# Attention probabilities in 384 columns instead of 512: the first 64 queries keep 64 keys, and their high and low parts share a transposed tile

## The chip, the core and the metric

The kernel runs on one core of a Trainium2 chip. TensorE does the matrix products, VectorE (DVE in the profile), ScalarE (ACT) and GpSimd (POOL) the elementwise work, and the DMA engines move and transpose data; SyncE (SP) issues nearly all DMAs. The metric is the device time of one execution in microseconds (us), lower is better.

## The reference

One transformer layer over 64 batch elements of 128 tokens and width 1024. Its input h comes from a token mixing stage (an S4 kernel) that isn't touched here. With `ln` for a layer norm:

```python
q = rope((ln(h) @ Wq).heads(32))          # head width 32
k = rope((ln(h) @ Wk).heads(8))           # 4 query heads share a key head
v = (ln(h) @ Wv).heads(8)
scores = q @ k.T / sqrt(32)
scores = where(key > query, lowest, scores)   # causal
h = h + softmax(scores) @ v @ Wo
logits = ln(h) @ Wr.T + br                # 8 experts of rank 16
h = h + 2 * einsum(ln(h) @ A.T, B, 8 * softmax(logits))
```

Since it is causal, the first 64 queries of an element see at most the first 64 keys.

## The kernel before

`s4_stage` makes h and stores it to HBM, and converts the weights. `layer_stage` does the layer, one batch element (128 tokens on the 128 partitions) at a time. Products are done in float16 with each operand split into a high part and a low part (the rounding's remainder), in three products: high with high, high with low, low with high.

Every engine runs its own list of steps, written out by hand: `body(i)` for i from -3 to 66, with steps for several elements at once (queries and keys of i+1 and i+2, attention of i, output projection of i-1, experts of i-2 and i-3). Nothing is reordered at run time: an engine takes its steps in this order, and each step first waits on semaphores (`reached`, `landed`). The order of TensorE's body is fixed in `body` at lines 1005 to 1048.

Attention goes by groups: group g (0 to 7) is one key head with its four query heads. Its steps are:

- `scores(b, g)`, TensorE, line 924: four matmuls into one PSUM bank. A tile is one half h of the queries (64) of a pair of heads, side by side on the 128 partitions. Tiles with h = 0 have 64 columns of keys, tiles with h = 1 have 128. `TILES` gives each of the four its place in a row of 512 columns.
- `mask_min`, VectorE, line 1207: mask and row minimum, tile by tile, into `pr`. It waits until `p_low` of group g - 2 has left `pr`.
- `exps`, ScalarE, line 1063: exponential and row sums, tile by tile.
- `reciprocals`, VectorE, line 1215: 1 / row sum, four a partition.
- `normalise`, GpSimd, line 1428: all 512 columns of `pr` times the reciprocals. Columns 64 to 127 of the h = 0 tiles hold zeros, set once.
- `p_high`, ScalarE, line 1073: the high part in float16 into `p16`; it waits (`landed`) until the DMA transpose of group g - 2 has read `p16`.
- `p_low`, GpSimd, line 1436: the low part, next to it.
- `p_transpose`, SyncE, line 862: a DMA transpose of the 1024 columns of `p16` into eight tiles `pt` of 128 x 128.
- `values(b, m)`, TensorE, line 939, twice an element, for groups 4m to 4m + 3: three rounds (v_hi with p high, v_lo with p high, v_hi with p low). A round has four matmuls of 512 columns, one a group, each with 32 weight columns on its own strip of 32 columns of the array. They add up in the bank `pv_ps`.
- `ctx_high` (ScalarE, line 1081) and `ctx_low` (VectorE, line 1221) split `pv_ps` into `ctx_t` (tiles 0 to 7 high, 8 to 15 low), which the output projection `wo_half` uses. Its blocks with k of 4 and more wait for `ctx_low(b, 1)`.

V itself comes from `kv_rotate` (VectorE) through `v_high` (ScalarE) and `v_low` (GpSimd, line 1476). Other steps named below: `norm_apply` (ScalarE, line 1099, a layer norm applied), `x_high` (ScalarE, line 1112) and `x_low` (VectorE, line 1268) split the activations; `sum_k` (GpSimd, line 1463) adds the two parts of the rotated keys; `q_double` and `k_double` (VectorE, lines 1307 and 1315) are float16 copies. In VectorE's body the steps around the change stand in this order:

```python
                    x_low(1, i - 2, 1)
                    mask_min(i, 3)
                    reciprocals(i, 2)
                    if i >= 0:
                        x_low(0, i + 2, 1)
                    reciprocals(i, 3)
                    ctx_low(i - 1, 1, 1 - odd)
```

and in GpSimd's, around the same time: `normalise` 0 and 1, `p_low` 0 and 1, `sum_k`, `normalise` 2 and 3, `p_low` 2 and 3.

Of the kernel before, what the change touches and what calls it, by code (L numbers as in the profile page):

```python
# [14 lines left out]
f16 = mybir.dt.float16  # L15
ALU = mybir.AluOpType
ACT = mybir.ActivationFunctionType
AX = mybir.AxisListType

P = 128  # L20
# [4 lines left out]
H, G, HD = 32, 8, 32  # L25
HG = H // G
# [8 lines left out]
RP = 4  # L35
# [31 lines left out]
HT = T // 2  # L67
# [574 lines left out]
def layer_stage(nc, h0, out, W, h_sent, ln_in):  # L642
# [5 lines left out]
    with ExitStack() as ctx:  # L648
        def sb(name, shape, dt=f32):
            return ctx.enter_context(nc.sbuf_tensor(name, shape, dt))  # L650

        def sem(name):
            return ctx.enter_context(nc.semaphore(name))

        def ps(name):
# [23 lines left out]
        ks = sb("ks", [P, G, 2, 2, HD], f16)  # L679
        kt = sb("kt", [P, G, P], f16)  # L680
        vf = sb("vf", [P, G * HD])
        v_hi = [sb(f"v_hi{i}", [P, G * HD], f16) for i in range(2)]
        v_lo = [sb(f"v_lo{i}", [P, G * HD], f16) for i in range(2)]
        smin = [sb(f"smin{i}", [P, HG]) for i in range(2)]
        pr = [sb(f"pr{i}", [P, HG * P]) for i in range(2)]
        rsum = [sb(f"rsum{i}", [P, HG]) for i in range(2)]
        rinv = [sb(f"rinv{i}", [P, HG]) for i in range(2)]
        p16 = [sb(f"p16{i}", [P, 2 * HG * P], f16) for i in range(2)]
        pt = [sb(f"pt{i}", [P, 2 * HG, P], f16) for i in range(RP)]
        ctx_t = [sb(f"ctx_t{i}", [P, 2 * G, P], f16) for i in range(2)]  # L690
        h1 = [W[f"rows{i}"][:, :, :].rearrange("p t l -> p (t l)") for i in range(2)]
        z8 = sb("z8", [P, NF])
# [10 lines left out]
        pv_ps, pa, pb, pc, pd, tx = (ps(n) for n in ("pv_ps", "pa", "pb", "pc", "pd", "tx"))  # L703
# [19 lines left out]
        ph_done = sem("ph_done")  # L723
# [9 lines left out]
        vh_done = sem("vh_done")  # L733
        masked = sem("masked")
        rinv_done = sem("rinv_done")
# [13 lines left out]
        k_sum = sem("k_sum")  # L749
        kl_done = sem("kl_done")  # L750
        vl_done = sem("vl_done")
        p_norm = sem("p_norm")

        TILES = tuple((h, pair, slice((2 * h + pair) * P, (2 * h + pair) * P + (HT, P)[h]))
                      for h in range(2) for pair in range(HG // 2))

        def in_halves(bank):
            return bank[:, :].rearrange("p (h j q) -> p h j q", h=2, j=HG)
# [1 line left out]
        def in_tokens(buf, k):  # L760
            return buf[:, k:k + HG, :].rearrange("p j (h q) -> p h j q", h=2)

        def has(b):
            return not isinstance(b, int) or 0 <= b < NB

        def reached(eng, s, per, b, k=0):

            if isinstance(b, int):
                if b < 0 or per * b + k == 0:
                    return  # L770
                if b >= NB:
                    b, k = NB, 0
            eng.wait_ge(s, per * b + k)
# [13 lines left out]
        with nc.Block() as block:  # L787
# [103 lines left out]
            def _(pe):  # L891
# [36 lines left out]
                def values(b, m, odd):  # L928
                    if not has(b):
                        return  # L930
                    if m == 0:
                        reached(pe, vl_done, 1, b, 1)
                    reached(pe, ctxl_done, G // 4, b, m)
                    for g in range(4 * m, 4 * m + 4):
                        landed(pe, b, g)
                    for n, (v, lo) in enumerate(((v_hi[odd], 0), (v_lo[odd], 0), (v_hi[odd], HG))):
                        for g in range(4 * m, 4 * m + 4):
                            strip = slice(HD * (g % 4), HD * (g % 4) + HD)
                            last = pe.matmul(pv_ps[strip, :], v[:, g * HD:(g + 1) * HD],  # L939
                                             pt[g % RP][:, lo:lo + HG, :], start=(n == 0), stop=(n == 2))  # L940
                    last.then_inc(pv_done, 1)

                def kv(b, odd, k0, k1):
# [110 lines left out]
            def _(act):  # L1054
# [12 lines left out]
                def p_high(b, g):  # L1067
                    if not has(b):
                        return
                    reached(act, p_norm, G, b, g + 1)  # L1070
                    pb_, pg = group(b, g - 2)
                    landed(act, pb_, pg)
                    A.activation(p16[g % 2][:, 0:HG * P], pr[g % 2][:, :], ACT.Copy).then_inc(ph_done, 1)  # L1073

                def ctx_high(b, m, odd):
                    if not has(b):
# [62 lines left out]
                def v_high(b, odd):  # L1139
                    if not has(b):  # L1140
                        return
                    reached(act, kv_used, 1, b, 1)
                    reached(act, pv_done, G // 4, b - 1)
                    A.activation(v_hi[odd][:, :], vf[:, :], ACT.Copy).then_inc(vh_done, 1)

                def router_exp(b):
                    if not has(b):
# [49 lines left out]
            def _(dve):  # L1197
# [13 lines left out]
                def reciprocals(b, g):  # L1211
                    if not has(b):
                        return
                    reached(dve, exp_done, G, b, g + 1)
                    V.reciprocal(rinv[g % 2][:, :], rsum[g % 2][:, :]).then_inc(rinv_done, 1)  # L1215

                def ctx_low(b, m, odd):
                    if not has(b):
                        return
                    reached(dve, ctxh_done, G // 4, b, m + 1)  # L1220
                    V.tensor_tensor(in_tokens(ctx_t[odd], G + 4 * m), in_halves(pv_ps),  # L1221
                                    in_tokens(ctx_t[odd], 4 * m), ALU.subtract).then_inc(ctxl_done, 1)

                def norm_half(w, src, b, half):
                    V.bn_stats(bn[w][:, 6 * half:6 * half + 6], src[:, 512 * half:512 * half + 512]).then_inc(ln_v[w], 1)
# [143 lines left out]
                def body(i, odd):  # L1369
# [3 lines that stand above are left out]
                    if i >= 0:  # L1373
                        x_low(0, i + 2, 1)
                    reciprocals(i, 3)
                    ctx_low(i - 1, 1, 1 - odd)
                    ls_low(i - 3)
                    mask_min(i, 4)
                    mask_min(i, 5)
                    reciprocals(i, 4)  # L1380
                    residual2(i - 3, 0, 1 - odd)
                    norm1_stats(i + 3)
                    residual2(i - 3, 1, 1 - odd)
                    reciprocals(i, 5)
                    q_double(i + 1, 0)
                    q_rotate(i + 1, 1)
                    residual1(i - 1, 0, 1 - odd)
                    mask_min(i, 6)
                    residual1(i - 1, 1, 1 - odd)
                    mask_min(i, 7)  # L1390
                    k_double(i + 1)
                    reciprocals(i, 6)
                    router_max(i - 2)
                    reciprocals(i, 7)
                    norm_refine(1, i - 1)
                    router_weights(i - 2)
                    norm_refine(0, i + 3)
                    if i == -3:
                        first_apply()
                    mask_min(i + 1, 0)  # L1400
                    mask_min(i + 1, 1)
                    q_double(i + 1, 1)
                    reciprocals(i + 1, 0)
                    x_low(1, i - 1, 0)
                    ctx_low(i, 0, odd)
                    reciprocals(i + 1, 1)
                    if i < -1:
                        x_low(0, i + 3, 0)
                        x_low(0, i + 3, 1)
                    kv_rotate(i + 2)  # L1410
                    q_rotate(i + 2, 0)
                    mask_min(i + 1, 2)
                    if i >= -1:
                        x_low(0, i + 3, 0)


                for i in range(2):
                    V.memset(pr[i][:, :].rearrange("p (t k) -> p t k", t=HG)[:, 0:2, HT:P], 0.0)
                bodies(dve, body)

            @block.gpsimd
            def _(pool):
                def normalise(b, g):
                    if not has(b):
                        return
                    reached(pool, rinv_done, G, b, g + 1)
                    p3 = pr[g % 2][:, :].rearrange("p (j k) -> p j k", j=HG)
                    nc.gpsimd.tensor_tensor(p3, p3, rinv[g % 2][:, :].unsqueeze(2).broadcast_to([P, HG, P]),  # L1428
                                            ALU.mult).then_inc(p_norm, 1)

                def p_low(b, g):
                    if not has(b):
                        return
                    reached(pool, ph_done, G, b, g + 1)
                    p = p16[g % 2]
                    nc.gpsimd.tensor_tensor(p[:, HG * P:], pr[g % 2][:, :], p[:, 0:HG * P],  # L1436
                                            ALU.subtract).then_inc(pl_done, 1)

                def sum_q(b, half):

# [31 lines left out]
                def v_low(b, odd):  # L1472
                    if not has(b):
                        return
                    reached(pool, vh_done, 1, b, 1)
                    nc.gpsimd.tensor_tensor(v_lo[odd][:, :], vf[:, :], v_hi[odd][:, :], ALU.subtract).then_inc(vl_done, 1)

                def body(i, odd):
                    v_low(i, odd)
# [59 lines left out]
```

## Time and profile before

| | |
|---|---|
| time, median of 3 runs | 2348.03 us (2345.55 to 2348.85) |
| the profiled execution | 2350.26 us, span 2348.1 us |
| granted TensorE clock, mean | 0.989 |
| TensorE busy | 2231.6 us, 95% |
| TensorE weight loads | 1147.6 us, 49% |
| VectorE busy | 1818.7 us, 77% |
| ScalarE busy | 1760.8 us, 75% |
| GpSimd busy | 1750.0 us, 75% |

The span is the time from the first to the last recorded instruction. The first stage takes some 250 us; from 330 to 2250 us the layer stage is full, one body after another. Matmuls are pipelined: the recorded duration of one is longer than its distance to the next, so distances between starts are what counts on TensorE. The other engines also begin an instruction some 0.1 us before the end of the one before it is recorded.

### The profile page before, as it was taken

The numbers are of one execution on the slowest core, as the hardware profiler recorded it, in microseconds if no ns is written. First come the engines' busy times: TensorE is split into PE (matmuls) and PEld (weight loads), VectorE is DVE, ScalarE is ACT, GpSimd is POOL, SyncE is SP. The second block draws the span as 40 slices with busy tenths as digits, with TensorE's granted clock in tenths as the row PEclk, the third lists the DMA queues.
The fourth block names the chain that finished last, engine by engine and source line by source line (L and its number), as shares of the span: only waits on it lengthen the run. The fifth ranks groups of instructions, "written<-read, shape, count | busy, mean of one in ns | idle before, by whom it ended". The sixth has DMA issues, their size and how long they took to land.

```text
span 2348.1 us, 49641 instructions
## 1 busy us (share of the span) xinstructions
PE 2231.6 (95%) x14040; PEld 1147.6 (49%) x14040; DVE 1818.7 (77%) x7750; ACT 1760.8 (75%) x6141; POOL 1750.0 (75%) x1550
## 2 busy tenths in 40 slices
PE   3898699999999999999999999999999999999986
PEld 2777344444444444444444444444444444444442
DVE  8999467777777777777777777877777777777864
ACT  5787477777787777777777777777778777778772
POOL 3776387777777778777778778788777777778772
PEclk9999899999999999999999999999999999999988
DMA  3888599999999999999999999999999999999994
GB/s 95 268 268 259 126 176 181 193 188 186 194 194 186 189 196 181 195 193 186 192 194 188 187 191 192 188 195 191 186 197 190 189 192 192 181 196 192 190 166 105
DMA packets 1205661, 443.10 MB, mean 189 GB/s; under 512 B 1155718, under 2 KB 1158022, under 8 KB 1205388
## 3 DMA queue, kind: packets, MB, share of 16 engines
q1 hardware_dynamic: 1205380, 439.93, 95.9%
q8 instruction: 113, 1.85, 0.3%
q14 instruction: 160, 1.31, 0.2%
q10 hardware_dynamic: 8, 0.01, 0.0%
HBM read 87.43 MB, written 67.11 MB: 66 GB/s over the span
## 4 chain that ended last, share of the span: by engine, by line
PE 67%; DMA 6%; POOL 6%; DVE 4%; SPq 3%; issue 2%; ACT 2%; POOLq 0%; DVEq 0%; ACTq 0%
PE pc L910 11%; PE pb L910 10%; PE pa L910 10%; DMA pt<-p 4%; PE pb L896 4%; PE pb L898 4%; PE pb L897 4%; PE pa L896 4%; PE pa L897 4%; PE pa L898 4%; PE pv_ps L939 3%; PE s_ps L924 3%; POOL p L1436 3%; POOL pr L1428 2%; DMA h_ln<-h 2%
## 5 line engine op out<-in xcount | busy, mean ns | idle before, releaser
L1063 ACT ACTIVATE pr<-pr,smin 128x64 f32<-128x64 f32 (+1 forms) x2048 | 738.8, 362 | 185.3 <-DVE smin L1207 184.4
L1428 POOL TENSOR_TENSOR pr<-pr,rinv 128x512 f32<-128x512 f32 x512 | 577.0, 1137 | 367.8 <-DVE rinv L1215 366.8
L1436 POOL TENSOR_TENSOR p<-pr,p 128x512 f16<-128x512 f32 x512 | 590.9, 1158 | 66.6 <-ACT p L1073 64.6
L1207 DVE CUSTOM_DVE_ANT_0 pr<-s_ps,cst 128x64 f32<-128x64 f32 (+1 forms) x2048 | 404.2, 252 | 219.0 <-PE s_ps L924 119.0
L1073 ACT ACTIVATE p<-pr 128x512 f16<-128x512 f32 x512 | 320.1, 625 | 257.8 <-DMA pt<-p 133.6
L1063 ACT ACTIVATION_READ_ACCUMULATOR pr<-pr,smin 128x1 f32 x2048 | 382.3, 187 | 0.0
L910 PE MATMUL pa<-wkv_hi,xt 128*128 128x512 f16 x1024 | 326.5, 380 | 13.4 <-DMA xt<-xs 13.4
L910 PE MATMUL pb<-wq_hi,xt 128*128 128x512 f16 x1024 | 326.9, 381 | 0.0
L910 PE MATMUL pc<-wq_hi,xt 128*128 128x512 f16 x1024 | 315.2, 379 | 0.0
L635 PE MATMUL hps<-z,xw 128*128 128x256 f32 x792 | 178.8, 386 | 60.5 <-POOL xw L363 38.2
L896 PE MATMUL pa<-wo_hi,ctx_t 128*128 128x512 f16 x512 | 195.5, 382 | 2.0 <-DVE ctx_t L1221 1.8
L910 PE MATMUL pb<-wq_lo,xt 128*128 128x512 f16 x512 | 195.4, 382 | 0.0
L897 PE MATMUL pa<-wo_lo,ctx_t 128*128 128x512 f16 x512 | 195.2, 381 | 0.0
L898 PE MATMUL pa<-wo_hi,ctx_t 128*128 128x512 f16 x512 | 195.2, 381 | 0.0
L910 PE MATMUL pa<-wkv_lo,xt 128*128 128x512 f16 x512 | 194.8, 381 | 0.0
L896 PE MATMUL pb<-wo_hi,ctx_t 128*128 128x512 f16 x512 | 194.7, 380 | 0.1
L898 PE MATMUL pb<-wo_hi,ctx_t 128*128 128x512 f16 x512 | 194.7, 380 | 0.0
L897 PE MATMUL pb<-wo_lo,ctx_t 128*128 128x512 f16 x512 | 194.7, 380 | 0.0
L910 PE MATMUL pc<-wq_lo,xt 128*128 128x512 f16 x512 | 194.2, 379 | 0.0
L635 PEld LDWEIGHTS hps<-z,xw 128*128 128x128 f32 x792 | 151.0, 193 | 87.9 <-POOL xw L363 44.2
L924 PEld LDWEIGHTS s_ps<-kt,qt 128*128 128x128 f16 x2048 | 121.8, 98 | 127.4 <-DVE smin L1207 22.5
L924 PE MATMUL s_ps<-kt,qt 128*128 128x64 f16 (+1 forms) x2048 | 172.0, 207 | 7.4 <-issue 4.1
(185 smaller groups left out, 4723.5 us busy)
## 6 DMA issues: line engine op xcount, KB each, us to landing
h<-rows SPq DMA_DIRECT2D x128, 256.0 KB, 4.0
h_res<-h SPq DMA_DIRECT2D x64, 512.0 KB, 4.6
out<-rows SPq DMA_DIRECT2D x64, 512.0 KB, 3.4
h_ln<-h SPq DMA_DIRECT2D x63, 512.0 KB, 4.5
pt<-p SPq DMA_TRANSPOSE x512, 4.1
xa<-x SPq DMA_DIRECT2D x16, 256.0 KB, 4.4
xb<-x SPq DMA_DIRECT2D x32, 128.0 KB, 3.8
wst<-wq SPq DMA_DIRECT2D x8, 512.0 KB, 4.9
```

Source lines behind the costliest of these rows:

```text
L635: last = pe.matmul(hps[t % 4][:, QROW * i:QROW * i + QROW], xw[w % XWR][:, t % WIN, 2 * i:2 * i + 2, :], z[g % ZR][:, 2 * (t % 2) + m, :], ...
L896: pe.matmul(bank, x[:, k, :], w_hi[:, k, cols], start=(k == 0), stop=False)
L897: pe.matmul(bank, x[:, k, :], w_lo[:, k, cols], start=False, stop=False)
L898: last = pe.matmul(bank, x[:, KC + k, :], w_hi[:, k, cols], start=False, stop=(k == KC - 1))
L910: last = pe.matmul(bank, x[:, k if n < 2 * KC else KC + k, :], w[:, k, cols], start=(n == 0), stop=(n == 3 * KC - 1))
L924: last = pe.matmul(s_ps[g % 2][:, cols], qt[h][:, head:head + 2, :], kt[:, g, 0:HT * h + HT], start=True, stop=True)
L939: last = pe.matmul(pv_ps[strip, :], v[:, g * HD:(g + 1) * HD], pt[g % RP][:, lo:lo + HG, :], start=(n == 0), stop=(n == 2))
L1063: last = A.activation(p, p, ACT.Exp, bias=smin[g % 2][:, j:j + 1], scale=-1.0, accum_out=rsum[g % 2][:, j:j + 1])
L1073: A.activation(p16[g % 2][:, 0:HG * P], pr[g % 2][:, :], ACT.Copy).then_inc(ph_done, 1)
L1207: V.tensor_tensor_reduce(pr[g % 2][:, cols], s_ps[g % 2][:, cols], masks[h], 1.0, 3e38, ALU.add, ALU.min, smin[g % 2][:, j:j + 1]).then_in ...
L1428: nc.gpsimd.tensor_tensor(p3, p3, rinv[g % 2][:, :].unsqueeze(2).broadcast_to([P, HG, P]), ALU.mult).then_inc(p_norm, 1)
L1436: nc.gpsimd.tensor_tensor(p[:, HG * P:], pr[g % 2][:, :], p[:, 0:HG * P], ALU.subtract).then_inc(pl_done, 1)
```

## The change

The probabilities are kept in 384 columns, six blocks of 64: block 0 is the h = 0 tile of the first pair of heads, blocks 1 to 4 are the two h = 1 tiles, block 5 is the h = 0 tile of the second pair. `normalise` works on six blocks with a reciprocal for each, so `reciprocals` writes each of its four values twice. `p_high` and `p_low` become two instructions each, one for the 256 columns of the h = 1 tiles, one for the two h = 0 blocks, of which the high and the low part are put side by side, 64 and 64 columns. So `p16` has 768 columns and `pt` six tiles: 0 and 1 high of h = 1, 2 and 3 low of h = 1, and 4 and 5 with h = 0, where the high part comes out on partitions 0 to 63 and the low part on 64 to 127.

`values` then has three rounds of 256 columns for h = 1 as before, and two rounds of 256 columns for h = 0. These use a copy of V whose first 64 tokens stand on both halves of the partitions (`v_twice`), so that one matmul adds the products with the high and the low part. `values_twice` makes it on VectorE, ahead of `ctx_low`, in two copies of 64 partitions.

```diff
-        TILES = tuple((h, pair, slice((2 * h + pair) * P, (2 * h + pair) * P + (HT, P)[h]))
-                      for h in range(2) for pair in range(HG // 2))
+        TILES = ((0, 0, slice(0, HT)), (1, 0, slice(HT, 3 * HT)),
+                 (1, 1, slice(3 * HT, 5 * HT)), (0, 1, slice(5 * HT, 6 * HT)))
+
+        def upper(p):
+            return p[:, HT:5 * HT]
+
+        def lower(p):
+            return p[:, :].rearrange("p (n k) -> p n k", k=HT)[:, 0:6:5, :]
+
+        def stacked(p, part):
+            return p[:, 4 * P:6 * P].rearrange("p (n s k) -> p n s k", s=2, k=HT)[:, :, part, :]
...
                     if m == 0:
-                        reached(pe, vl_done, 1, b, 1)
+                        reached(pe, vt_done, 1, b, 1)
...
-                    for n, (v, lo) in enumerate(((v_hi[odd], 0), (v_lo[odd], 0), (v_hi[odd], HG))):
-                        for g in range(4 * m, 4 * m + 4):
-                            strip = slice(HD * (g % 4), HD * (g % 4) + HD)
-                            last = pe.matmul(pv_ps[strip, :], v[:, g * HD:(g + 1) * HD],
-                                             pt[g % RP][:, lo:lo + HG, :], start=(n == 0), stop=(n == 2))
+                    for rounds, cols in ((((v_hi[odd], 0), (v_lo[odd], 0), (v_hi[odd], 2)), slice(2 * P, 4 * P)),
+                                         (((vt_hi[odd], 4), (vt_lo[odd], 4)), slice(0, 2 * P))):
+                        for n, (v, tile) in enumerate(rounds):
+                            for g in range(4 * m, 4 * m + 4):
+                                strip = slice(HD * (g % 4), HD * (g % 4) + HD)
+                                last = pe.matmul(pv_ps[strip, cols], v[:, g * HD:(g + 1) * HD],
+                                                 pt[g % RP][:, tile:tile + 2, :],
+                                                 start=(n == 0), stop=(n == len(rounds) - 1))
...
-                    A.activation(p16[g % 2][:, 0:HG * P], pr[g % 2][:, :], ACT.Copy).then_inc(ph_done, 1)
+                    A.activation(p16[g % 2][:, 0:2 * P], upper(pr[g % 2]), ACT.Copy).then_inc(ph_done, 1)
+                    A.activation(stacked(p16[g % 2], 0), lower(pr[g % 2]), ACT.Copy).then_inc(ph_done, 1)
...
-                    V.reciprocal(rinv[g % 2][:, :], rsum[g % 2][:, :]).then_inc(rinv_done, 1)
+                    V.reciprocal(rinv[g % 2][:, :, :],
+                                 rsum[g % 2][:, :].unsqueeze(2).broadcast_to([P, HG, 2])).then_inc(rinv_done, 1)
...
+                def values_twice(b, odd):
+                    if not has(b):
+                        return
+                    reached(dve, vl_done, 1, b, 1)
+                    V.tensor_copy(v_twice[odd][0:HT, :, :], v_parts[odd][0:HT, :, :])
+                    V.tensor_copy(v_twice[odd][HT:P, :, :], v_parts[odd][0:HT, :, :]).then_inc(vt_done, 1)
...
                     reciprocals(i, 3)
+                    values_twice(i, odd)
                     ctx_low(i - 1, 1, 1 - odd)
...
-                    p3 = pr[g % 2][:, :].rearrange("p (j k) -> p j k", j=HG)
-                    nc.gpsimd.tensor_tensor(p3, p3, rinv[g % 2][:, :].unsqueeze(2).broadcast_to([P, HG, P]),
+                    p3 = pr[g % 2][:, :].rearrange("p (n k) -> p n k", k=HT)
+                    by_block = rinv[g % 2][:, :, :].rearrange("p j s -> p (j s)")[:, 1:7]
+                    nc.gpsimd.tensor_tensor(p3, p3, by_block.unsqueeze(2).broadcast_to([P, 6, HT]),
                                             ALU.mult).then_inc(p_norm, 1)
...
-                    nc.gpsimd.tensor_tensor(p[:, HG * P:], pr[g % 2][:, :], p[:, 0:HG * P],
-                                            ALU.subtract).then_inc(pl_done, 1)
+                    p, q = p16[g % 2], pr[g % 2]
+                    reached(pool, ph_done, 2 * G, b, 2 * g + 1)
+                    nc.gpsimd.tensor_tensor(p[:, 2 * P:4 * P], upper(q), p[:, 0:2 * P], ALU.subtract)
+                    reached(pool, ph_done, 2 * G, b, 2 * g + 2)
+                    nc.gpsimd.tensor_tensor(stacked(p, 1), lower(q), stacked(p, 0), ALU.subtract).then_inc(pl_done, 1)
```

## Rows read from the trace of the kernel before

**Rows 1.** Windows: busy us (instructions) of each engine, granted clock, DMA share, GB/s.
```profile
330.00:2250.00 1920.00, 1914.67 (x12443) 933.15 (x12442) 1486.95 (x7027) 1488.45 (x5350) 1512.45 (x1385) 1.00 1.02 190
2250.00:2349.00 99.00, 67.75 (x430) 32.06 (x427) 52.44 (x229) 46.82 (x176) 42.01 (x39) 0.84 0.63 125
```

**Rows 2.** Timeline of TensorE's matmuls, one body: start, us, instruction [idle before].
```profile
2153.23 0.33 PE L924 MATMUL s_ps<-kt,qt 128*128 128x64 f16 x4
...
2159.13 0.40 PE L939 MATMUL pv_ps<-pt,v_hi 128*32 128x512 f16 x4
...
2159.57 0.39 PE L939 MATMUL pv_ps<-pt,v_hi 128*32 128x512 f16 x4
2159.89 0.34 PE L924 MATMUL s_ps<-kt,qt 128*128 128x64 f16 x4
...
2165.42 0.38 PE L896 MATMUL pa<-wo_hi,ctx_t 128*128 128x512 f16 x1
```

**Rows 3.** Timeline of TensorE's weight loads in the same call of values.
```profile
2159.14 0.10 PEld L939 LDWEIGHTS pv_ps<-pt,v_lo 128*32 128x32 f16 x4
```

**Rows 4.** Timeline of VectorE in the same body.
```profile
2160.42 0.81 DVE L1268 TENSOR_TENSOR xs<-h_ln,xs 128x512 f16<-128x512 f32 x1
2161.15 1.21 DVE L1268 TENSOR_TENSOR xs<-xn,xs 128x512 f16<-128x512 f32 x1
...
2163.09 0.65 DVE L1268 TENSOR_TENSOR xs<-h_ln,xs 128x512 f16<-128x512 f32 x1
2164.11 0.18 DVE L1215 RECIPROCAL rinv<-rsum 128x4 f32<-128x4 f32 x1 [0.37 <-ACT pr L1063]
2164.21 0.66 DVE L1221 TENSOR_TENSOR ctx_t<-pv_ps,ctx_t 128x512 f16<-128x512 f32 x1
```

**Rows 5.** Timeline of ScalarE in the same body.
```profile
2157.15 0.63 ACT L1073 ACTIVATE p<-pr 128x512 f16<-128x512 f32 x1 [0.30 <-POOL pr L1428]
...
2158.82 0.61 ACT L1073 ACTIVATE p<-pr 128x512 f16<-128x512 f32 x1
2159.34 1.04 ACT L1112 ACTIVATE xs<-h_ln 128x1024 f16<-128x1024 f32 x1
2160.29 0.33 ACT L1063 ACTIVATE pr<-pr,smin 128x64 f32<-128x64 f32 x1
...
2162.54 0.35 ACT L1063 ACTIVATE pr<-pr,smin 128x64 f32<-128x64 f32 x1 [0.24 <-DVE smin L1207]
...
2165.59 0.26 ACT L1158 ACTIVATE ls_hi<-tx 128x128 f16<-128x128 f32 x1
```

**Rows 6.** Timeline of GpSimd in the same body (x2: two in a row).
```profile
2152.17 0.68 POOL L1476 TENSOR_TENSOR v_lo<-vf,v_hi 128x256 f16<-128x256 f32 x1
...
2155.72 2.45 POOL L1428 TENSOR_TENSOR pr<-pr,rinv 128x512 f32<-128x512 f32 x2 [1.76 <-DVE rinv L1215]
...
2159.52 1.17 POOL L1436 TENSOR_TENSOR p<-pr,p 128x512 f16<-128x512 f32 x1 [0.21 <-ACT p L1073]
2160.64 1.17 POOL L1463 TENSOR_TENSOR kr<-kt_c,kt_s 128x256 f32<-128x256 f32 x1
2163.24 2.40 POOL L1428 TENSOR_TENSOR pr<-pr,rinv 128x512 f32<-128x512 f32 x2 [1.43 <-DVE rinv L1215]
```

**Rows 7.** Single lines over the whole run: duration ns min/median/max, first and last start.
```profile
L1428 POOL TENSOR_TENSOR pr<-pr,rinv x512: 1029/1040/1413, 278.8 to 2304.8; 128x512 f32<-128x512 f32 x171
...
L1463 POOL TENSOR_TENSOR kr<-kt_c,kt_s x64: 726/1174/1182, 264.6 to 2255.8; 128x256 f32<-128x256 f32 x64
...
L1315 DVE COPY ks<-ks x64: 287/291/1036, 273.3 to 2274.9; 128x512 f16<-128x512 f16 x64
...
L1144 ACT ACTIVATE v_hi<-vf x64: 398/400/403, 265.7 to 2263.2; 128x256 f16<-128x256 f32 x64
```

**Rows 8.** Waits: engine, line, waited for, us in total, times, longest.
```profile
ACT p L1073 <- DMA pt<-p: 133.6, 169, 2.6
```

**Rows 9.** The transposes of p16, from issue to landing.
```profile
DMA to landing us min/median/max: 3.0/4.1/7.0
```

More of the change, by code:

```diff
@@ L681, in layer_stage @@
         vf = sb("vf", [P, G * HD])
-        v_hi = [sb(f"v_hi{i}", [P, G * HD], f16) for i in range(2)]
-        v_lo = [sb(f"v_lo{i}", [P, G * HD], f16) for i in range(2)]
+        v_parts = [sb(f"v_parts{i}", [P, 2, G * HD], f16) for i in range(2)]
+        v_twice = [sb(f"v_twice{i}", [P, 2, G * HD], f16) for i in range(2)]
+        v_hi, v_lo = ([a[:, n, :] for a in v_parts] for n in range(2))
+        vt_hi, vt_lo = ([a[:, n, :] for a in v_twice] for n in range(2))
         smin = [sb(f"smin{i}", [P, HG]) for i in range(2)]
-        pr = [sb(f"pr{i}", [P, HG * P]) for i in range(2)]
+        pr = [sb(f"pr{i}", [P, 6 * HT]) for i in range(2)]
         rsum = [sb(f"rsum{i}", [P, HG]) for i in range(2)]
-        rinv = [sb(f"rinv{i}", [P, HG]) for i in range(2)]
-        p16 = [sb(f"p16{i}", [P, 2 * HG * P], f16) for i in range(2)]
-        pt = [sb(f"pt{i}", [P, 2 * HG, P], f16) for i in range(RP)]
+        rinv = [sb(f"rinv{i}", [P, HG, 2]) for i in range(2)]
+        p16 = [sb(f"p16{i}", [P, 6 * P], f16) for i in range(2)]
+        pt = [sb(f"pt{i}", [P, 6, P], f16) for i in range(RP)]
         ctx_t = [sb(f"ctx_t{i}", [P, 2 * G, P], f16) for i in range(2)]
@@ L751, in layer_stage @@
         vl_done = sem("vl_done")
+        vt_done = sem("vt_done")
         p_norm = sem("p_norm")
-        TILES = tuple((h, pair, slice((2 * h + pair) * P, (2 * h + pair) * P + (HT, P)[h]))
-                      for h in range(2) for pair in range(HG // 2))
+        TILES = ((0, 0, slice(0, HT)), (1, 0, slice(HT, 3 * HT)),
[6 more added lines that the diff above has]
+            return p[:, 4 * P:6 * P].rearrange("p (n s k) -> p n s k", s=2, k=HT)[:, :, part, :]
         def in_halves(bank):
@@ L1143, in v_high @@
                     reached(act, pv_done, G // 4, b - 1)
-                    A.activation(v_hi[odd][:, :], vf[:, :], ACT.Copy).then_inc(vh_done, 1)
+                    A.activation(v_hi[odd], vf[:, :], ACT.Copy).then_inc(vh_done, 1)
                 def router_exp(b):
@@ L1414, in body @@
                         x_low(0, i + 3, 0)
-                for i in range(2):
-                    V.memset(pr[i][:, :].rearrange("p (t k) -> p t k", t=HG)[:, 0:2, HT:P], 0.0)
                 bodies(dve, body)
@@ L1433, in p_low @@
                         return
-                    reached(pool, ph_done, G, b, g + 1)
-                    p = p16[g % 2]
-                    nc.gpsimd.tensor_tensor(p[:, HG * P:], pr[g % 2][:, :], p[:, 0:HG * P],
-                                            ALU.subtract).then_inc(pl_done, 1)
+                    p, q = p16[g % 2], pr[g % 2]
[3 more added lines that the diff above has]
+                    nc.gpsimd.tensor_tensor(stacked(p, 1), lower(q), stacked(p, 0), ALU.subtract).then_inc(pl_done, 1)
                 def sum_q(b, half):
@@ L1475, in v_low @@
                     reached(pool, vh_done, 1, b, 1)
-                    nc.gpsimd.tensor_tensor(v_lo[odd][:, :], vf[:, :], v_hi[odd][:, :], ALU.subtract).then_inc(vl_done, 1)
+                    nc.gpsimd.tensor_tensor(v_lo[odd], vf[:, :], v_hi[odd], ALU.subtract).then_inc(vl_done, 1)
                 def body(i, odd):
```

## The prediction

> **What bounds the kernel now.** I read the windows first, the 1920 us in which the layer stage runs full against the rest: TensorE is busy 1914.67 us of them at the full granted clock (1.00, the 2.4 GHz level), VectorE, ScalarE and GpSimd 77 to 79% each [rows 1]. So the kernel costs what TensorE's own stream costs, plus 5.3 us in which it visibly stood; only the last 99 us are a chain of waits. There are 64 bodies, one per batch element, and their work on TensorE is fixed by the written order. Two questions remain: what the change takes from that stream, and which wait reaches TensorE once the stream is shorter.
>
> For the second I went through the timeline of one undisturbed body, engine by engine, and looked for what TensorE would wait for next. All times below are us behind its first scores at 2153.23 [rows 2]. The order is a chain. ScalarE's `p_high(0)` begins at 3.92, released by GpSimd's `normalise(0)`; then ScalarE is occupied without a break: a layer norm, `p_high(1)` at 5.59, `x_high`, `exps(2)` at 7.06, `ctx_high`, `exps(3)` at 9.31, which waited 0.24 for the mask of group 3 [rows 5]. VectorE can take the reciprocal of group 3 only then, at 10.88, and `ctx_low` at 10.98, which ends at 11.64 [rows 4]. TensorE's fifth `wo` block (k = 4) needs that result: it begins at 12.19, and a weight load may be as late as some 0.05 before its matmul, so the real slack is 12.19 - 0.05 - 11.64 = 0.50 [rows 2, 4]. Everything that the change puts in front of `ctx_low` has to fit in there.
>
> **The change part by part.** *Values.* Today a call is three rounds of four matmuls of 512 columns; the four lie on four column strips and start together, and the rounds follow at 0.22 (0.44 between the first and the third start, [rows 2]). 512 columns at 2.4 GHz are 213 ns. After it a call is three rounds of 256 columns and two more of 256: five rounds of 109 ns, 546 ns for 648. The switch before and after the call (0.32 from the third round to the next scores, 0.10 more than a round, [rows 2]) stays. Saved: 0.102 us a call, 128 calls, **-13.1 us**. This asks that four weight loads fit in 109 ns: four recorded loads take 0.10 together [rows 3]. The upper bound for a round is a load and then a start, 0.13, which makes 5 x 0.13 = 0.65: nothing saved. I take the lower, since the four loads of the first round did not hold up the matmuls at 2159.13.
>
> The Trainium skill (TensorE: Matmul & The Clock Gate, LDWEIGHTS) puts a load at its columns / 1.2 GHz, 27 ns for 32 columns. One after another four would make 107 ns, still within a round, and the estimate by it is the same saving.
>
> *GpSimd.* `normalise` goes over 384 columns for 512. Alone it takes 1.04 [rows 7]; 256 columns took 0.68 in `v_low` [rows 6], `sum_k` 0.73 at its least [rows 7], so some 0.18 are fixed and 384 columns make 0.83 (bounds: 0.78, three quarters of 1.04, and 1.04). Where it was held back by VectorE it ended 0.90 behind the end of VectorE's instruction (2163.24 + 2.40 - 1.04 = 2164.60 against 2163.09 + 0.65, [rows 4, 6]); now 0.68. `p_low`, 1.17, becomes two of 256 and 128 columns: 0.67 + 0.43. Off TensorE's path in itself.
>
> *ScalarE.* `p_high` of 512 columns takes 0.61 to 0.63 and holds the engine 0.52 (2158.82 to 2159.34); 256 columns take 0.40 and 128 take 0.26 [rows 5, 7], each some 0.09 less in a stream: 0.31 + 0.20 = 0.51. No more than before, and the first half is out 0.2 earlier.
>
> *VectorE.* The reciprocal writes 8 elements for 4: some 0.03 more, 512 times, bounded by nothing and 0.17, a second one. `mask_min` and `exps` keep their shapes, in another order that begins with 64 columns as before. Two copies (`values_twice`) are new, each 512 float16 a partition; such a copy takes 0.29 alone [rows 7]. They stand right before `ctx_low`, past the reciprocal that ScalarE releases, with nothing to cover them.
>
> *The transposes.* 512 DMA transposes go from 8 to 6 tiles. They land after 4.1, at times 7.0 [rows 9]; a quarter off is some 1 us. ScalarE waited 133.6 us in 169 places for them [rows 8], as `p_high` may not overwrite `p16` before; when that falls on `p_high(0)`, the whole chain above slips, and the slack runs out. Issue also comes earlier with GpSimd's shorter pieces. I book 4.5 of the 5.3 us of visible stalls as gone (bounds 0 and 5.3): **-4.5**.
>
> *What the copies cost on the path.* The rows show who shares what. `x_low` at 2160.42 lasted 0.81 where its twin lasts 0.65: it started under a `p_low` that ended at 2160.69, and ended 0.54 behind it. The next one lasted 1.21, behind `sum_k`, and `sum_k`, issued between the two, took 1.17 instead of 0.73 [rows 4, 6, 7]. So an operation of one engine waits for that of the other to end, and they alternate: the one of GpSimd that waits goes ahead of VectorE's next. Copies wait too: 0.29 as a rule, up to 1.04 [rows 7].
>
> The Trainium skill (SBUF — State Buffer, Who interferes with whom) says that VectorE's fast copies and GpSimd take a shared pair of ports as an exclusive lock for a whole instruction; the trace agrees. By that rule a copy is only cheap where GpSimd is idle, which speaks against this place; without the rule, at 0.29 a copy, the sum would be that of the second case below, with it that of the forecast.
>
> The chain anew: `normalise(0)` ends at 3.70 (3.89 less 0.22, plus 0.03 for the reciprocal), `p_high(0)` 3.73, `p_high(1)` 5.37, `exps(2)` 6.83. `p_low(1)` ends at 6.85, `sum_k` runs to 7.52 ahead of `x_low`, the two `x_low` end at 8.07 and 8.65, mask 3 begins at 8.57, `exps(3)` at 8.82, the reciprocal at 10.40: 0.48 earlier than before. The third `x_low` of the body, which begins at 9.86 [rows 4] today and keeps its distance to mask 3, ends at 10.05, and `normalise(2)` behind it at 10.72; the first copy waits for it and ends at 10.87. `normalise(3)`, free since the reciprocal, waits and goes next, to 11.55; the second copy ends at 11.70, `ctx_low` runs from 11.62 to 12.28, and the `wo` block can start at 12.34. It is due at 12.19 - 0.10 = 12.09. **A new stall of 0.25 us a body**, in some 60 bodies: **+15**. If `normalise` takes 0.78, three of them in the chain take off 0.15 and the stall is 0.10 (+6); if 0.90, it is 0.46 (+28). If the second copy gets in ahead of `normalise(3)`, there is none.
>
> *The ends.* In the last 99 us TensorE is busy 67.75 [rows 1], the rest is the last element's chain with its eight transposes and GpSimd steps: two of the waits for them should shrink by about 1.2 each, **-2.5** (bounds 0 and -5).
>
> Sum: -13.1 - 4.5 + 15 - 2.5 = -5.1 us. The profiled execution took 2350.26 (span 2348.10 and 2.16 around it), 0.1% above the median 2348.03; from the median it gives **2343 us**.
>
> **The rivals.** *The copies slip through* (the second goes ahead of GpSimd, or GpSimd's pieces are shorter than I think): no stall, 2348 - 13 - 4.5 - 2.5 = 2328, at best 2326. For it: the chain itself is 0.48 earlier, about what the two copies take when nobody stands in the way (0.4). Against it: the order of `x_low`, `sum_k`, `x_low`.
>
> *The copies lose more* (slower than before): each waits for a whole GpSimd operation, or `normalise` doesn't shrink with its columns. From a stall of 0.35 a body on the saving is eaten up: 2348 - 20 + 60 x 0.35 = 2349; with 0.5 it is 2358, with 0.9 (a `normalise` still at 1.04) 2382.
>
> *No gain on TensorE*: rounds of 256 columns bound by their loads at 0.13. Then the stream is as long as before, the due time is 12.19 and the stall 0.15: 2348 - 7 + 9 = 2350. For it is only that four loads are recorded as 0.10, so close to the round. Were a round of 256 as long as one of 512, it would be 128 x 0.43 = 55 us slower; the recorded starts give no reason for that.
>
> **How the numbers follow.** About 0.2% (4.7 us) is what a measurement of this kernel can tell from no change, so the bounds are 2343.3 and 2352.7. Chances: the forecast (stall 0.1 to 0.35, 2334 to 2350) 0.47, and it lies on both sides of the first bound, 0.26 and 0.21; the copies slip through 0.25, all faster; they lose more 0.20, nearly all slower; no gain on TensorE 0.08, half same, half slower. Together faster 0.51, same 0.26, slower 0.23. The range of 2327 to 2358 leaves out the best corner of the second case and the worst of the third. The likeliest case's own range is 2334 to 2350.
>
> **What would show it.** Rounds of `values` 0.11 apart. GpSimd's `normalise` at 0.83 alone. The first copy of a body longer than 0.29, the second some 0.8, with a `normalise` between them. `ctx_low` 11.6 behind the first scores and the fifth `wo` block's load waiting for it: that wait, now a few us, should be some 15 us over the run. ScalarE's wait for the transposes far below 133.6. I am wrong if the `wo` block does not wait (then the time is near 2328), or if the wait is over 20 us.

## The result: 2362.6 us, slower by 0.61%

The changed kernel takes 2362.6 us (median of 6 runs, 2361.62 to 2365.24) beside 2348.44 us of the kernel before in the same comparison: ratio 1.0061, 95% interval 1.005 to 1.0072. 2343 us and a small gain were forecast, so the direction is wrong too. The profiled execution has a span of 2362.8 us.

From the changed kernel's profile: busy time of each engine over the whole run, and the windows (busy us and instructions of TensorE's matmuls, its weight loads, VectorE, ScalarE, GpSimd; granted clock; DMA share; GB/s) of the full stretch and of the end.

```profile
PE 2227.8 (94%) x15064; PEld 1178.7 (50%) x15064; DVE 1876.9 (79%) x7876; ACT 1752.0 (74%) x6653; POOL 1571.8 (67%) x2062
```
```profile
330.00:2262.00 1932.00, 1907.75 (x13383) 959.66 (x13382) 1539.13 (x7136) 1478.54 (x5823) 1342.14 (x1865) 1.00 0.93 172
2262.00:2363.00 101.00, 70.36 (x488) 35.91 (x486) 54.65 (x241) 48.11 (x195) 37.85 (x57) 0.83 0.57 118
```

GpSimd gave back 178 us of its work, and the DMA engines are no longer full (0.93 for 1.02). TensorE's busy time fell from 2231.6 to 2227.8, and yet it stands for 24 us of the full stretch where it stood for 5 [rows 1]. ScalarE has as much to do as before, in more pieces. Every engine was lightened or left as it was, except VectorE (1876.9 us for 1818.7), and the time went into a wait. The timelines of one body tell which. Its first scores are at 2134.56; TensorE's matmuls first (start, us, instruction, idle before it and its releaser; `...` marks lines left out).

```profile
2134.56 0.33 PE L936 MATMUL s_ps<-kt,qt 128*128 128x64 f16 x4
...
2140.46 0.51 PE L953 MATMUL pv_ps<-pt,v_parts 128*32 128x256 f16 x12
2140.79 0.39 PE L953 MATMUL pv_ps<-pt,v_twice 128*32 128x256 f16 x8
2141.12 0.34 PE L936 MATMUL s_ps<-kt,qt 128*128 128x64 f16 x4
...
2147.14 0.39 PE L908 MATMUL pa<-wo_hi,ctx_t 128*128 128x512 f16 x1 [0.33 <-DVE ctx_t L1238]
```

The three rounds of 256 columns take 0.33, 0.11 each, and from the first matmul of the call to the next scores it is 0.66 where it was 0.76 [rows 2]. But the fifth `wo` block, the last line above, begins 12.58 behind the first scores instead of 12.19, and waits for `ctx_low`. VectorE, GpSimd and ScalarE in the same body:

```profile
2141.51 1.19 DVE L1292 TENSOR_TENSOR xs<-h_ln,xs 128x512 f16<-128x512 f32 x1
2142.63 0.68 DVE L1292 TENSOR_TENSOR xs<-xn,xs 128x512 f16<-128x512 f32 x1
2143.23 0.21 DVE L1223 CUSTOM_DVE_ANT_0 pr<-s_ps,cst 128x64 f32<-128x64 f32 x1
...
2145.06 0.20 DVE L1231 RECIPROCAL rinv<-rsum 128x8 f32<-128x8 f32 x1 [0.37 <-ACT pr L1078]
2145.18 0.34 DVE L1245 COPY v_twice<-v_parts 64x512 f16<-64x512 f16 x1
2145.53 0.82 DVE L1246 COPY v_twice<-v_parts 64x512 f16<-64x512 f16 x1
2146.39 0.69 DVE L1238 TENSOR_TENSOR ctx_t<-pv_ps,ctx_t 128x512 f16<-128x512 f32 x1
```
```profile
2141.04 0.43 POOL L1462 TENSOR_TENSOR p<-pr,p 128x128 f16<-128x128 f32 x1
2141.43 0.73 POOL L1488 TENSOR_TENSOR kr<-kt_c,kt_s 128x256 f32<-128x256 f32 x1
2144.21 2.00 POOL L1452 TENSOR_TENSOR pr<-pr,rinv 128x384 f32<-128x384 f32 x2 [2.05 <-DVE rinv L1231]
2146.17 0.71 POOL L1460 TENSOR_TENSOR p<-pr,p 128x256 f16<-128x256 f32 x1
```
```profile
2138.28 0.42 ACT L1088 ACTIVATE p<-pr 128x256 f16<-128x256 f32 x1
2138.60 0.29 ACT L1089 ACTIVATE p<-pr 128x128 f16<-128x128 f32 x1
...
2143.48 0.35 ACT L1078 ACTIVATE pr<-pr,smin 128x64 f32<-128x64 f32 x1
```

The chain to the reciprocal is faster than before, as forecast: `p_high(0)` at 3.72 (before 3.92), `exps(3)` at 8.92 (9.31), the reciprocal at 10.50 (10.88) [rows 4, 5]. Then come the two copies, 0.34 and 0.82, and `ctx_low` starts at 11.83 (10.98). From the start of the reciprocal to that of `ctx_low` it was 0.10, and now it is 1.33. The second copy ends at 2146.35, just behind the second of the two `normalise`, which end at 2146.21: that `normalise` runs while the copy is recorded.

Single lines of the changed kernel over the whole run (ns min/median/max): the second copy and `normalise`. Then its transposes of `p16`, and its waits (us in total, times, longest):

```profile
L1246 DVE COPY v_twice<-v_parts x64: 822/824/893, 287.0 to 2303.7; 64x512 f16<-64x512 f16 x64
```
```profile
L1452 POOL TENSOR_TENSOR pr<-pr,rinv x512: 821/831/1168, 279.3 to 2318.2; 128x384 f32<-128x384 f32 x171
```
```profile
DMA to landing us min/median/max: 2.7/3.7/7.1
```
```profile
ACT p L1088 <- DMA pt<-p: 64.9, 73, 2.9
...
PEld pa L908 <- DVE ctx_t L1238: 33.9, 62, 1.5
PE pa L908 <- DVE ctx_t L1238: 24.9, 61, 1.4
```

The kernel before had these waits of TensorE for `ctx_low` and for the transposes:

```profile
PEld pa L896 <- DVE ctx_t L1221: 3.3, 8, 0.6
PE pv_ps L939 <- DMA pt<-p: 15.5, 7, 4.4
```

The second copy is as slow in all 64 bodies, and TensorE waits for `ctx_low` in 61 or 62 of them. The stall itself can be read from starts: the fifth `wo` block begins 0.17 behind the scores ahead of it where nothing waits. What it is later than that, added up over the bodies, is 35.0 us in 62 bodies, and was 3.4 us in 12 bodies before.

### The profile page after: what moved, and what is told of

Read it like the earlier page. It is cut to its first block, busy times and chain, and to the rows that moved or that the text cites. A ratio compares the mean times of both kernels' runs of the same rounds, so it can differ in the third digit from the quotient of the medians.

```text
span 2362.8 us, 52839 instructions
## 1 busy us (share of the span) xinstructions
PE 2227.8 (94%) x15064; PEld 1178.7 (50%) x15064; DVE 1876.9 (79%) x7876; ACT 1752.0 (74%) x6653; POOL 1571.8 (67%) x2062
## 4 chain that ended last, share of the span: by engine, by line
PE 52%; DVE 12%; ACT 11%; issue 7%; POOL 4%; DMA 4%; SPq 1%; ACTq 0%; POOLq 0%; DVEq 0%
PE pb L922 8%; PE pa L922 8%; PE pc L922 7%; ACT pr L1078 5%; PE pb L908 3%; PE pb L910 3%; PE pb L909 3%; DVE pr L1223 3%; POOL pr L1452 3%; PE pa L908 3%; DMA pt<-p 3%; ACT xs L1128 2%; PE pa L909 2%; PE pa L910 2%; DVE v_twice L1246 2%
## 5 line engine op out<-in xcount | busy, mean ns | idle before, releaser
L1078 ACT ACTIVATE pr<-pr,smin 128x128 f32<-128x128 f32 (+1 forms) x2048 | 738.8, 362 | 214.9 <-DVE smin L1223 208.7
L1452 POOL TENSOR_TENSOR pr<-pr,rinv 128x384 f32<-128x384 f32 x512 | 470.7, 924 | 572.8 <-DVE rinv L1231 565.5
L1223 DVE CUSTOM_DVE_ANT_0 pr<-s_ps,cst 128x128 f32<-128x128 f32 (+1 forms) x2048 | 403.2, 252 | 169.4 <-PE s_ps L936 136.2
L1460 POOL TENSOR_TENSOR p<-pr,p 128x256 f16<-128x256 f32 x512 | 346.5, 677 | 33.5 <-ACT p L1088 28.6
L1088 ACT ACTIVATE p<-pr 128x256 f16<-128x256 f32 x512 | 209.7, 410 | 198.3 <-POOL pr L1452 126.0
L1462 POOL TENSOR_TENSOR p<-pr,p 128x128 f16<-128x128 f32 x512 | 218.6, 427 | 0.0
L936 PEld LDWEIGHTS s_ps<-kt,qt 128*128 128x128 f16 x2048 | 135.9, 98 | 114.0 <-DVE smin L1223 15.4
```

Of the source, the lines that this page charges most:

```text
L936: last = pe.matmul(s_ps[g % 2][:, cols], qt[h][:, head:head + 2, :], kt[:, g, 0:HT * h + HT], start=True, stop=True)
L1078: last = A.activation(p, p, ACT.Exp, bias=smin[g % 2][:, j:j + 1], scale=-1.0, accum_out=rsum[g % 2][:, j:j + 1])
L1088: A.activation(p16[g % 2][:, 0:2 * P], upper(pr[g % 2]), ACT.Copy).then_inc(ph_done, 1)
L1223: V.tensor_tensor_reduce(pr[g % 2][:, cols], s_ps[g % 2][:, cols], masks[h], 1.0, 3e38, ALU.add, ALU.min, smin[g % 2][:, j:j + 1]).then_in ...
L1452: nc.gpsimd.tensor_tensor(p3, p3, by_block.unsqueeze(2).broadcast_to([P, 6, HT]), ALU.mult).then_inc(p_norm, 1)
L1460: nc.gpsimd.tensor_tensor(p[:, 2 * P:4 * P], upper(q), p[:, 0:2 * P], ALU.subtract)
```

## The experiments

In all of them the ratio is to the kernel before, run on the same chip. Its median was 2353.55 us beside the first four kernels below and 2347.31 us beside the other four. Neither times nor ratios are exact across the two groups: five kernels below that hardly wait for `ctx_low` have times of 2327.3 to 2330.6 us in either group, but ratios of 0.9895 to 0.9937. Differences of some 6 us between the groups are therefore not told apart here. Stalls read from the starts, as above, are given where they settle it.

**The copies taken away** (no_copies). The doubled V is zeroed once, so the attention of the first 64 queries is left out. `values` waits for `v_low` and for the zeroing, and no longer for the copies.

```diff
-                        reached(pe, vt_done, 1, b, 1)
+                        reached(pe, vl_done, 1, b, 1)
+                        pe.wait_ge(vt_done, 2)
...
                     reciprocals(i, 3)
-                    values_twice(i, odd)
                     ctx_low(i - 1, 1, 1 - odd)
...
+                for i in range(2):
+                    V.memset(v_twice[i][:, :, :], 0.0).then_inc(vt_done, 1)
                 bodies(dve, body)
```

> The changed kernel without the two copies of V in the loop: the doubled V is set to zero once ahead of it, so the attention of the first 64 queries is left out of the result; every other instruction of the change stays. Theory A (the copies ahead of ctx_low are the whole loss): the fifth wo block does not wait, TensorE's 35 us of stalls there go, 2362.6 - 33 = about 2330 us. Theory B (the loss is in the change's other parts, the pieces on ScalarE and GpSimd or TensorE's rounds, and the copies only lie on top of it): the wait stays or another takes its place, 2345 us or more.

2330.62 us, ratio 0.9911 (0.9895 to 0.9927). `ctx_low` starts at 10.62, TensorE's fifth `wo` block at 12.08, where 12.09 was said to be due, and the stall is 0.9 us over the run. Theory A holds and B falls: what is left of the change, with more pieces on ScalarE and GpSimd and rounds of 256 columns, is a gain of some 20 us, and the two copies turned it into the loss.

**The copies behind `ctx_low`** (behind_ctx).

```diff
                     reciprocals(i, 3)
-                    values_twice(i, odd)
                     ctx_low(i - 1, 1, 1 - odd)
+                    values_twice(i, odd)
```

> The changed kernel with values_twice right behind ctx_low instead of ahead of it, nothing else. Theory A: ctx_low starts some 10.6 us behind the first scores instead of 11.8, is done 0.7 us before it is due, and the time is that of the kernel without the copies within 2 us, 2328 to 2332 us. The copies now hold back mask_min of group 4, which waits for p_low of group 2 until about the same time anyway. Theory C (the cost moves with the copies: the next steps of VectorE are as tight): scores or out_half wait instead, 2340 us or more.

2328.95 us, ratio 0.9902 (0.9885 to 0.9918), the same as with no copies. The copies themselves stay slow there (medians 0.58 and 0.67), but the stall is 1.4 us.

**The copies behind the reciprocals of group 4** (later).

```diff
                     reciprocals(i, 4)
+                    values_twice(i, odd)
                     residual2(i - 3, 0, 1 - odd)
```

> The changed kernel with values_twice behind the reciprocals of group 4, ahead of the second residual, where VectorE waits for TensorE's expert product anyway. Theory A: as with the copies right behind ctx_low, 2328 to 2332 us, the copies hidden in that wait. Theory C: 2340 us or more.

2327.91 us, ratio 0.9895 (0.9881 to 0.991): 1% faster than the kernel before. Its full stretch, its second copy over the whole run, and its waits:

```profile
330.00:2228.00 1898.00, 1897.19 (x13380) 957.83 (x13379) 1535.20 (x7133) 1478.50 (x5823) 1339.23 (x1864) 1.00 0.95 175
```
```profile
L1246 DVE COPY v_twice<-v_parts x64: 823/842/894, 290.6 to 2274.0; 64x512 f16<-64x512 f16 x64
```
```profile
PE pa L908 <- DVE ctx_t L1238: 1.0, 2, 0.5
```

The second copy is just as slow here, 0.84, behind another `normalise`. It costs nothing in the full stretch, since VectorE's next step waits for TensorE even so, and TensorE stands for 0.8 us of 1898. Both places refute theory C: what made the copies dear was who stands in line behind them.

**The copies ahead of the reciprocal** (ahead_recip). This asks why the second copy takes 0.82 and not 0.29.

```diff
-                    reciprocals(i, 3)
                     values_twice(i, odd)
+                    reciprocals(i, 3)
                     ctx_low(i - 1, 1, 1 - odd)
```

> The changed kernel with values_twice ahead of the reciprocals of group 3, so that GpSimd has no released operation left when the second copy comes. Theory A1 (what makes the copies dear is that normalise(3), released by that reciprocal, gets in between them): the first copy waits for normalise(2), the second takes 0.3 us instead of 0.82, ctx_low starts at about 11.2 instead of 11.83 and the wo block does not wait: 2329 to 2334 us. Theory A2 (the copies take 1.3 us wherever they stand, for their partitions or their form): ctx_low at 11.45 or later, a stall of 0.1 to 0.3 us a body, 2336 to 2350 us.

2339.39 us, ratio 0.9946 (0.9931 to 0.9961). VectorE and GpSimd in one body (first scores at 2111.67):

```profile
2121.17 0.64 DVE L1292 TENSOR_TENSOR xs<-h_ln,xs 128x512 f16<-128x512 f32 x1
2121.72 0.91 DVE L1245 COPY v_twice<-v_parts 64x512 f16<-64x512 f16 x1
2122.65 0.29 DVE L1246 COPY v_twice<-v_parts 64x512 f16<-64x512 f16 x1
2122.97 0.20 DVE L1231 RECIPROCAL rinv<-rsum 128x8 f32<-128x8 f32 x1
2123.09 0.64 DVE L1238 TENSOR_TENSOR ctx_t<-pv_ps,ctx_t 128x512 f16<-128x512 f32 x1
```
```profile
2121.33 1.16 POOL L1452 TENSOR_TENSOR pr<-pr,rinv 128x384 f32<-128x384 f32 x1 [2.06 <-DVE rinv L1231]
2123.25 0.83 POOL L1452 TENSOR_TENSOR pr<-pr,rinv 128x384 f32<-128x384 f32 x1 [0.76 <-DVE rinv L1231]
```

The same copy takes 0.29, as no `normalise` has been released that could go between; the first one waits for the `normalise` that runs (to 2122.49) and takes 0.91. A1 holds on the instruction, but not on the time, which lies above its 2334 us and in the range of A2: `ctx_low` starts at 11.42 and not 11.2, the `wo` block at 12.11 instead of 12.08. The typical body just makes it, and has no slack left; the bodies in which ScalarE's `p_high` steps are late pass it on. By the starts the stalls are 9 us in 50 bodies, and 8 of these 9 us lie in 14 bodies in which `p_high(1)` was 0.2 to 1.5 us late. What decides against A2 is the second copy's 0.29 here and the run before_copies below.

**One copy instead of two** (one_copy). The copy to partitions 64 to 127 stays; the lower half of the doubled V is zeroed once, so the products with the high parts of the first 64 queries are left out.

```diff
-                    V.tensor_copy(v_twice[odd][0:HT, :, :], v_parts[odd][0:HT, :, :])
                     V.tensor_copy(v_twice[odd][HT:P, :, :], v_parts[odd][0:HT, :, :]).then_inc(vt_done, 1)
...
+                for i in range(2):
+                    V.memset(v_twice[i][:, :, :], 0.0)
```

> The changed kernel with only the second of the two copies in the loop (partitions 64 to 127); the lower half of the doubled V is zeroed once, so the product of the first 64 queries' high parts is left out. Theory A (a copy waits for the GpSimd operation under way, and the second is dear only because normalise(3) goes between): the one copy ends at about 10.95, ctx_low starts at 11.0, is done 0.4 us before it is due, and the time is 2328 to 2333 us. Theory D (the copy to the other partitions is slow by itself, 0.8 us): ctx_low at about 11.5, no slack left, 2340 us or more.

2330.22 us, ratio 0.9937 (0.9922 to 0.9952). The ratio is less of a gain than no copies had, and the time is within 1 us of it; the stall is 0.9 us in both, so the difference in ratio is that of the two medians of the kernel before. The copy and what follows it:

```profile
2114.10 0.29 DVE L1245 COPY v_twice<-v_parts 64x512 f16<-64x512 f16 x1
2114.42 0.69 DVE L1238 TENSOR_TENSOR ctx_t<-pv_ps,ctx_t 128x512 f16<-128x512 f32 x1
```

The copy to the other half of the partitions takes 0.29 and `ctx_low` starts at 11.05, as A has it. D falls: 0.82 is not the price of moving data across partitions.

**The kernel before, with only the copies added** (before_copies).

```diff
                     reciprocals(i, 3)
+                    values_twice(i, odd)
                     ctx_low(i - 1, 1, 1 - odd)
```

The doubled V and its semaphore are added with it, and `values` waits for the copies; the trace has no such wait of TensorE.

> The kernel before, with only the doubled V added: values_twice with its two copies ahead of ctx_low, the copy not used by any matmul. Theory A (each copy waits for a normalise of GpSimd, here the long one of 512 columns, and the chain to ctx_low starts later than in the changed kernel, at 10.88 instead of 10.50): ctx_low starts at about 12.5 behind the first scores, the wo block waits 1.0 us or more a body, +60 to +85 us over the kernel before. Theory A2 (the copies cost the same 1.3 us in any surroundings): ctx_low at 12.2, a stall of 0.7 us a body, +45 us.

2418.31 us, ratio 1.0312 (1.0297 to 1.0327), +71 us on its chip. One body (first scores at 2187.87):

```profile
2198.85 0.58 DVE L1230 COPY v_twice<-v_parts 64x512 f16<-64x512 f16 x1
2199.44 1.03 DVE L1231 COPY v_twice<-v_parts 64x512 f16<-64x512 f16 x1
2200.50 0.69 DVE L1223 TENSOR_TENSOR ctx_t<-pv_ps,ctx_t 128x512 f16<-128x512 f32 x1
```
```profile
2197.88 2.44 POOL L1438 TENSOR_TENSOR pr<-pr,rinv 128x512 f32<-128x512 f32 x2 [1.43 <-DVE rinv L1217]
```
```profile
PEld pa L898 <- DVE ctx_t L1223: 79.0, 62, 2.3
```

Both copies grow with the `normalise` of 512 columns: 0.58 and 1.03 for 0.34 and 0.82. `ctx_low` starts at 12.63, the `wo` block at 13.38, 1.19 late. What a copy of the same size costs goes by GpSimd's operation, and A2, which had 45 us, falls.

**Four buffers for p16** (before_p16x4 and later_p16x4), in the kernel before and in the best one.

```diff
-        p16 = [sb(f"p16{i}", [P, 2 * HG * P], f16) for i in range(2)]
+        p16 = [sb(f"p16{i}", [P, 2 * HG * P], f16) for i in range(RP)]
...
-                    pb_, pg = group(b, g - 2)
+                    pb_, pg = group(b, g - RP)
```

> The kernel before with p16 in four buffers instead of two, so that p_high waits for the transpose of group g - 4 and not of g - 2. If the bodies in which ctx_low came late before were late because p_high(0) waited for a transpose, their stalls go: 3 to 7 us faster than before. If they have another cause, no change.

2343.51 us, ratio 0.9986 (0.9977 to 0.9995): 0.14% or 3 us. ScalarE's wait for the transposes, 133.6 us before [rows 8], is gone from the waits, and so is the stall at the fifth `wo` block, 3.4 us before: those bodies were late because ScalarE waited for a transpose. TensorE's own wait for a late transpose ahead of `values` is not gone (13.5 us, 9 times; 15.5 before):

```profile
  PE pv_ps L939: 13.5, 9
```

> The kernel with values_twice behind the reciprocals of group 4, with four p16 buffers too. There TensorE hardly waits any more in the full bodies, so 0 to 3 us less than with two buffers; against the kernel before with four buffers it should be 13 us for the values and 2 to 3 us at the end faster, 15 to 17 us.

2327.28 us, ratio 0.992 (0.9906 to 0.9934); in time within 1 us of two buffers, which ran in the other group, so a difference of a few us isn't excluded. TensorE's stall for `ctx_low` is 1.2 us with two buffers and none with four, so there is hardly anything left for them to give. To the kernel before with four buffers, on the same chip, it is 16 us less, as expected. The 2 to 3 us that the expectation puts at the end are not seen in the two traces, which take 118.1 and 119.2 us from the scores ahead of the fifth `wo` block of the third body from the end.

## Why the prediction was wrong

*The values' rounds*: right. 0.102 a call was forecast, three rounds take 0.33 and a call 0.10 less; weight loads do not bind these rounds of 256 columns, and the rival without a gain on TensorE falls.

*GpSimd and ScalarE*: right but for 0.10 at the end of the chain. `normalise` alone is 0.83, `p_high` 0.42 and 0.29 recorded with 0.32 and 0.20 between starts, and the chain to the reciprocal (`p_high(0)`, `p_high(1)`, `exps(2)`, `exps(3)`, reciprocal) came out at 3.72, 5.37, 6.82, 8.92 and 10.50, against 3.73, 5.37, 6.83, 8.82 and 10.40. There is some luck in the 0.83: the fixed part of 0.18 does not follow from the figures beside it, since 0.68 for 256 columns and 1.04 for 512 would make 0.32 fixed and 0.86 for 384. And the 0.90 by which `normalise` ended behind VectorE is what the trace has (2164.64), while the sum written for it gives 0.86.

*What the copies cost on the path*: the step that failed, by its size and not by its mechanism. `normalise(3)` did go between the copies: the second copy took 0.82 or more in every body. A stall of 0.25 was forecast, +15 us in all; the `wo` block starts at 12.58, and the run without copies shows it due at 12.08, so it is 0.49 or 0.50. Of the missing 0.24, 0.10 is the chain ahead of the reciprocal (`sum_k` started at 6.87 and not 6.79, and the two `x_low` ended 0.07 and 0.10 later); 0.11 is the passage from the copy to `ctx_low`, which I let overlap by 0.08 as after most VectorE instructions, while it starts 0.04 behind the copy's end; and 0.03 is `ctx_low` itself, 0.69 for 0.66. Three terms in a row were a little too low, and their sum counts in each of 62 bodies: +15 was written, 62 x 0.49 = 30 came, and 35.0 with the late bodies, of which 3.4 were there before.

The Trainium skill (SBUF — State Buffer, Who interferes with whom) calls the shared pair of ports an exclusive lock that is held for a whole instruction. The runs agree: the same copy took 0.29, 0.82 or 1.03, by whether an operation of GpSimd came first, and which.

*The transposes* (-4.5): right in part. Of the 5.3 us in which TensorE visibly stood before, 3.0 were four waits for a transpose ahead of `values`, and the changed kernel has none of them in its full stretch. ScalarE's wait for them fell from 133.6 to 64.9 us, though they land after 3.7 where a whole 1 us less than 4.1 was assumed. But the stall for `ctx_low` that late transposes had caused, 3.4 us before, did not go, as the kernels with four buffers show it could: where the slack is used up, a late chain passes on in full.

*The ends* (-2.5): nothing came. Outside the 58 bodies that are compared below, both kernels take 495.9 and 495.8 us. The kernels without the wait do not settle what the term is worth: from the scores ahead of the fifth `wo` block of the third body from the end they take 116.0 to 119.6 us, where the kernel before takes 119.3, and the short ones are those with the higher granted clock in that stretch (0.89 and 0.88 against 0.85).

In sum, between the scores ahead of the fifth `wo` block of the third body and those of the third body from the end, the 58 bodies went from 1852.3 to 1866.9 us. That is +14.7, the whole difference of the two spans. In it are 58 x -0.202 = -11.7 for the values, +29.3 for the stall for `ctx_low` (32.5 for 3.2 in this stretch), and -3.0 for the waits ahead of `values`: +14.6.

The rival "the copies lose more" is what happened; I put it at 2358 for a stall of 0.5, since I left it the gains of the transposes and the ends. The sign that the text gave for being wrong, a wait for `ctx_low` of more than 20 us, is there (33.9 us by the loads).

## What to carry to other kernels

An instruction put into a full schedule costs what the engines that wait behind it lose, and that can be nothing. In this kernel the same two copies cost some 34 us in front of `ctx_low` (the difference of the stalls) and nothing five steps later, so the place is worth as much care as the operation. Where the forecast is a slack minus a sum and the rest is repeated in every body, each 0.1 us of the sum is 6 us of the result: take start-to-start distances of the very pair of instructions, and a range that covers their sum.

## What was not expected of the hardware

VectorE's copy of 512 float16 on 64 partitions takes 0.23 to 0.25 within the same partitions and 0.29 to the other 64 when no operation of GpSimd is in its way, and 0.82 or 1.03 with a whole `normalise` of 384 or 512 columns ahead of it. When both engines have an operation waiting they take turns, as far as these timelines show in the order in which they asked.

These copies also do not overlap with the instruction behind them. The next one started 0.01 behind the first copy's end and 0.03 behind the second's, where most of VectorE's instructions overlap the next by 0.08. Copies on all 128 partitions do overlap, as `q_double` in the same body shows, so it is not a property of copies as such; what makes the difference is not shown.

```profile
2136.47 0.42 DVE L1331 COPY qs<-qs 128x1024 f16<-128x1024 f16 x1
2136.81 0.20 DVE L1231 RECIPROCAL rinv<-rsum 128x8 f32<-128x8 f32 x1
```
